# Block-local attention: the order in which SyncE moves keys, row maxima and queries of a group

## What is computed

```python
# B=8 batches, T=1024 tokens, C=128, H=16 heads of D=8, blocks of W=64 tokens, nb=16
q, k, v = (x @ Wq.T), (x @ Wk.T), (x @ Wv.T)       # split in 16 heads, 16 blocks of 64
k2 = concatenate([previous block of k, kb], axis=3) # 128 keys for 64 queries
v2 = concatenate([previous block of v, vb], axis=3)
base = (j > i) & (j <= i + W)                       # a sliding window of 64
scores = einsum('bhnqd,bhnkd->bhnqk', qb, k2) * D ** -0.5
p = softmax(where(mask, scores, -1e30), axis=-1)
out = einsum('bhnqk,bhnkd->bhnqd', p, v2)
x = x + out @ Wo.T
```

## Time and profile before

| | |
|---|---|
| median of 3 runs | 1809.45 us (1808.23 to 1809.67) |
| the profiled execution | 1814.3 us, of which the span is 1812.5 us |
| granted TensorE clock, mean of the span | 0.967 |
| PE busy | 1670.4 us, 92% of the span |
| DVE, ACT, POOL busy | 1393.8, 1137.5, 1177.3 us |
| the attention stage | from 73.6 us (first scores) to about 480 us |

### The profile page before, as it was taken

One profiled execution on the slowest core, in us unless ns is written; L12 is line 12 of the kernel. 1 busy time (PEld: TensorE's weight loads), 2 busy tenths in 40 slices (PEclk: granted clock), 3 DMA queues, 4 the chain that ended last, 5 costly groups with the idle time before them and its releaser, 6 DMA issues.

```text
span 1812.5 us, 39662 instructions
## 1 busy us (share of the span) xinstructions
PE 1670.4 (92%) x15057; PEld 1223.0 (67%) x15057; DVE 1393.8 (77%) x2976; ACT 1137.5 (63%) x2222; POOL 1177.3 (65%) x909
## 2 busy tenths in 40 slices
PE   4679999999877899999999999999999999999995
PEld 4557777777766567666766766766676677677674
DVE  5557777766597888878888888888887888888862
ACT  5447777777676466666666666666656666665662
POOL 4300111000066498898898988989889898898892
PEclk9889999999887899999999999999999999999997
DMA  4556666654000000000000000001001000100101
GB/s 123 136 140 156 162 156 159 164 136 116 29 1 1 1 10 8 10 8 10 7 13 16 10 8 19 11 7 22 7 10 19 8 10 7 22 7 10 19 10 30
DMA packets 198677, 81.47 MB, mean 45 GB/s; under 512 B 152553, under 2 KB 177493, under 8 KB 198357
## 3 DMA queue, kind: packets, MB, share of 16 engines
q1 hardware_dynamic: 198484, 78.93, 19.5%
HBM read 39.79 MB, written 29.88 MB: 38 GB/s over the span
## 4 chain that ended last, share of the span: by engine, by line
PE 54%; DVE 11%; POOL 2%; issue 1%; ACT 1%; DMA 0%; SPq 0%; POOLq 0%; ACTq 0%
PE pair L1825 12%; PE pair L1878 11%; PE pair L1882 11%; PE pair L1936 10%; DVE amax L1833 4%; PE pair L1929 4%; PE pair L1650 2%; DVE o_inv L1946 1%; PE pair L1641 1%; DVE stats L485 1%; POOL w_mix L1907 1%; PE pair L1664 1%; DVE q_low L1754 1%; DVE cq L1765 1%; DVE key_hl L1768 1%
## 5 line engine op out<-in xcount | busy, mean ns | idle before, releaser
L1893 ACT ACTIVATE prob<-pair 128x512 f32<-128x512 f32 x1024 | 604.4, 597 | 422.2 <-PE pair L1882 359.6
L1833 DVE TENSOR_REDUCE amax<-pair 128x1 f32<-128x512 f32 x1024 | 670.3, 682 | 133.9 <-PE pair L1825 131.8
L1825 PE MATMUL pair<-key_hl,q_hi 128*128 128x512 f32 x1024 | 437.8, 430 | 11.2 <-DVE amax L1833 7.1
L1878 PE MATMUL pair<-q_hi,key_hl 128*128 128x512 f32 x1024 | 405.2, 396 | 2.6 <-ACT prob L1893 2.6
L1882 PE MATMUL pair<-q_low,key_h 65*128 65x512 f32 x1024 | 406.0, 396 | 0.0
L1907 POOL TENSOR_TENSOR w_mix<-w_mix,prob 128x1024 f32<-128x1024 f32 x160 | 382.3, 2389 | 25.2 <-ACT prob L1893 8.5
L1907 POOL TENSOR_TENSOR Wm<-Wm,prob 128x1024 f32<-128x1024 f32 x155 | 369.6, 2384 | 20.8 <-ACT prob L1893 4.1
L520 POOL TENSOR_SCALAR veps<-mv 128x8 f32<-128x8 f32 x47 | 11.4, 243 | 452.6 <-DVE mv L493 451.2
L1825 PEld LDWEIGHTS pair<-key_hl,q_hi 128*128 128x128 f32 x1024 | 196.1, 192 | 115.9 <-issue 51.0
L1936 PE MATMUL pair<-prob,values 128*32 128x256 f32 x4096 | 247.2, 382 | 0.0
L1186 DVE TENSOR_REDUCE mx_neg<-pair 128x4 f32<-128x512 f32 x256 | 164.9, 687 | 94.8 <-PE pair L1090 94.1
(11 more groups left out here) (209 smaller groups left out, 2232.8 us busy)
## 6 DMA issues: line engine op xcount, KB each, us to landing
rows_mem<-once SPq DMA_DIRECT2D x128, 128.0 KB, 2.0
queries<-rows_mem SPq DMA_DIRECT2D x64, 256.0 KB, 4.5
keys<-rows_mem SPq DMA_DIRECT2D x16, 1024.0 KB, 7.1
rows_mem<-once SPq DMA_DIRECT2D x128, 64.0 KB, 1.9
q_low<-shift_cols SPq DMA_DIRECT2D x512, 0.5 KB, 2.0
yT<-o_norm SPq DMA_DIRECT2D x256, 32.0 KB, 1.9
x<-x_dram SPq DMA_DIRECT2D x8, 512.0 KB, 7.3
out_dram<-x SPq DMA_DIRECT2D x7, 512.0 KB, 3.4
```

The source lines that it names most:

```text
L1825: e.matmul(row_bank(("row", r, i)), q_hi[:, k, t * P:(t + 1) * P], key_hl[:, b % 2, i * HALF:(i + 1) * HALF], start=True, stop=True, skip_ ...
L1833: e.tensor_reduce(amax1[:, u % 2, t, i:i + 1], row_bank(("row", r, i)), AX_X, ALU.max).then_inc(*row_maxed.up((r, i)))
L1878: e.matmul(bank(j), key_hl[:, b % 2, ks], q_hi[:, k, sl], start=True, stop=False, skip_group_check=True)
L1893: e.activation(prob1[:, g % P_BUFS, half * HALF:(half + 1) * HALF], bank(K_BANKS[(2 * g + half) % 3]), ACT.Exp, scale=SCALE1).then_inc(*ke ...
```

## The change

Four edits.

- `window_plan`: of the two `once` parts of a group the keys' (i = 1) comes first, and the queries' (i = 0) second. The places in the plan stay.
- `sync`: for each hb now the spread and the gather of keys, then the maxima of group hb-2, then the spread and the gather of queries. For hb = 2 the maxima of group 0 come ahead of the keys. The loop runs one turn longer, so that the last maxima are moved.
- `sync_gather`: for keys of batch 2 and above, the wait names the last key rows that read the half that is overwritten. For half 1 (odd hb) that is the last step of group hb-4, as before; for half 0 (even hb) it is the first step of group hb-3, where it was that group's last.
- `opening`: the same swap for group 0.

```diff
@@ window_plan
-        [("turn", 0, 0), ("turn", 0, 1), ("once", 0, 0), ("once", 0, 1), ("v", 0, 0)])]
+        [("turn", 0, 0), ("turn", 0, 1), ("once", 0, 1), ("once", 0, 0), ("v", 0, 0)])]
...
-            first += [("once", after, i) for i in range(2)]
+            first += [("once", after, i) for i in (1, 0)]
@@ sync_gather
             elif b >= 2:
-                e.wait_ge(*key_rows.at(2 * HB * (2 * (b - 2) + 2) - 1))
+                e.wait_ge(*key_rows.at(2 * (HB * (hb - 4) + (HB if half == 0 else HB - 1)) + 1))
@@ sync
-            for hb in range(2 * B + 1):
+            for hb in range(2 * B + 2):
+                if hb == 2:
+                    sync_move_maxima(e, 0)
                 if hb < 2 * B:
-                    for i in range(2):
-                        sync_spread(e, hb, i)
-                    for i in range(2):
-                        sync_gather(e, hb, i)
-                if hb:
-                    sync_move_maxima(e, hb - 1)
+                    sync_spread(e, hb, 1)
+                    sync_gather(e, hb, 1)
+                if hb > 2:
+                    sync_move_maxima(e, hb - 2)
+                if hb < 2 * B:
+                    sync_spread(e, hb, 0)
+                    sync_gather(e, hb, 0)
```

## The result

The changed kernel takes 1924.48 us, the median of 4 runs (1912.33 to 1930.86), against 1808.84 us (1808.01 to 1809.67) for the kernel before: 1.0621 times as long, 95% interval 1.0587 to 1.0655. That is 115.6 us more, where 93 were forecast. The time lies inside the range of 1868 to 1935.

The account below looks back on a forecast made before the run. TensorE was taken to bound the kernel, busy 1670.4 of 1812.5 us. 12 x (6.2 + 2.9) = 109.2, less 4.0, 10.6 and 2.9, plus 1.4, gave +93 us: 1903 us, range 1868 to 1935.

Parts of the forecast that it names:

- The mechanism: On SyncE's queue maxima come behind keys' spread, landing and gather; TensorE waits in third steps, clock falls; +93 us, chance 0.80.
- The rival that the new order costs by itself: Not in the prediction; follow-up theory that early keys and swapped products slow the attention stage: above 1850 us; no chance given.
- The side of the gain: Rival: keys land before each group's start, so their waits and clock losses go; about 1787 or 1796 us; chance 0.05.
- the waits: TensorE's third step, groups 4 to 15: 12 waits for maxima of 6.2 us each, bounds 5.3 and 8.0.
- the clock: Behind each wait for maxima TensorE runs at the low level, costing 2.9 us; bounds 0 and 3.3.
- groups 1 and 2: At these groups' starts each spread has its own landing wait: 1.4 us lost together, bounds 0 and 3.
- the short waits: VectorE gets ahead during long waits, which takes perhaps 4 of the 5.8 us of TensorE's short waits away.
- waits for keys gone: TensorE's waits for keys of groups 4 to 15 disappear: 10.6 us won.
- the fifth step of the example: At group 5, four maxima moves follow the keys' gather and land at 208.6 to 209.2; 208.9 us taken.
- The other steps: SyncE at group 5: wait for `once`, eight spreads (4.06 us), landing 2.0 us from issue, keys' gather issue 1.26 us.
- My argument that both waits above 2.7 us were followed by it: Against the rival without clock loss (chance 0.08, about 1867 us): waits of 4.18 and 2.73 us preceded the low level.
- the rival: Worse than the high end: queries also land after the next group's start, using 7 us slack; above 1935 us; chance 0.04.

Follow-up runs that it names:

- both_spreads: Changed kernel with SyncE's order per group made maxima first, then the keys' and queries' spreads, then both gathers; 1811.39 us, 1.0013 of the kernel before.
- pool_moves: Changed kernel's order of keys and queries on SyncE, but GpSimd issues the four moves of each group's maxima; 1820.38 us, 1.0067 of the kernel before.
- pool_before: Kernel before with one change: GpSimd, not SyncE, moves the maxima; queries first, both spreads ahead of both gathers; 1806.48 us, ratio 0.9966.
- maxima_first: Changed kernel with the maxima of group hb-2 ahead of the keys of group hb for every hb, queries last; 1844.93 us, 1.0193 of the kernel before.
- maxima_landed: Changed kernel with the maxima moved after the landing of the keys' spread and ahead of the keys' gather; 1884.19 us, 1.0403 of the kernel before.
- pool_best: Changed kernel with GpSimd moving the maxima, and both spreads ahead of both gathers for groups 0 to 2; 1813.19 us, 1.003 of the kernel before.
- act_moves: Changed kernel's order of keys and queries on SyncE, but ScalarE issues the maxima's moves after copying them; 1832.82 us, 1.0118 of the kernel before.

## Why the prediction was right, and which terms were off

The mechanism was right: twelve waits, in each group's third step, for maxima that stand behind the keys' spread, landing and gather, and the low clock behind each. The rival that the new order costs by itself has only a small part: keys first costs nothing (both_spreads, 1.0013), and the change's whole order of spreads and gathers, with the maxima taken out of the queue, costs 11 of the 116 us (pool_moves, 1.0067). The side of the gain needed the keys' part to be through before the maxima were due; it began only 0.7 us after they were ready. The sum, 93, was a fifth below the 115.6 us measured: its three terms of cost (the waits, the clock, groups 1 and 2) were all too small, and only the short waits, where the gain was too small, went the other way. The mean wait lay inside its bounds; the clock and groups 1 and 2 did not. The sizes, term by term, against the 115.0 us between the two spans:

| term | forecast | measured | |
|---|---|---|---|
| 12 waits for the maxima | 74.4 | 88.9 | 7.4 us each, not 6.2 |
| clock, less group 12's old loss | 31.9 | 39.4 | more busy time of the same matmuls |
| waits for keys gone | -10.6 | -11.0 | 9.4, 0.4 for maxima and 1.2 at group 15 |
| short waits gone | -4.0 | -7.6 | 5.0 and 3.7 before, 1.1 after |
| groups 1 and 2 | 1.4 | 5.1 | group 3's start |
| sum | 93.1 | 114.8 | |

- **The wait: the fifth step of the example was too short.** I had the maxima land 5.3 us after the issue of the keys' gather, with the keys there after 5.2 us by the lone load. They came 6.2 to 7.0 us after it (304.07 to 310.28, and 233.65 to 240.64 at group 5's place), 6.5 in the mean of the twelve. That is the whole difference of 1.2 us. The keys themselves landed after 5.3 to 6.0 us, mean 5.6, which is near the load; the last of the four moves could be used 0.9 us behind them in the mean, while I let the two end together. The other steps were good to some tenths: spread 298.47 to 302.56, landing wait 1.5 us.
- **Short waits**: those on VectorE fell by 4.1 us, as forecast. The 3.5 us on ScalarE's `yT` that went with them are the part that I had not counted.
- **The clock** cost (39.4 + 2.9) / 12 = 3.5 us a wait, group 12's old loss counted in, where I took 2.9 and 3.3 as the upper end. Its price varies. Read in stretches of 1 us, the low level went on for 12.9 to 13.2 us behind five of the twelve waits (groups 3, 4, 5, 6 and 9), and for 3.2 to 5.6 us behind the other seven, 7.9 us in the mean, where I had said about 6. These are the stretches after group 4's wait and after group 7's:

```profile
202.98:209.00 6.02, 6.02 (x64) 4.85 (x65) 1.29 (x2) 3.52 (x8) 0.00 (x0) 0.50 0.56 135
209.00:216.00 7.00, 7.00 (x68) 5.30 (x66) 3.20 (x10) 3.70 (x10) 0.00 (x0) 0.50 0.45 91
...
310.28:316.00 5.72, 5.72 (x66) 4.51 (x66) 1.21 (x2) 2.09 (x4) 0.00 (x0) 0.59 0.61 146
316.00:322.00 6.00, 6.00 (x92) 5.24 (x91) 5.14 (x15) 4.37 (x11) 0.00 (x0) 1.00 0.51 105
```

  The changed kernel's four runs differ by 18.5 us. The four of the kernel before beside them differ by 1.7, but the 19 runs of it in the comparison with pool_before differ by 14.4, so that this says little. The mean granted clock goes with the time (0.932 in the run of 1931 us, 0.931 in that of 1929, 0.938 in that of 1920 and 0.939 in that of 1912), but which waits made the difference stays open, since only one of the runs has a profile with these rows. Nor does the length of a wait alone decide: 2.73 us at group 12 of the kernel before was followed by the low level, 3.25 us at group 8 of maxima_first by 1.00 from 284.2 to 290.0 us. My argument that both waits above 2.7 us were followed by it rested on two rows.
- **Groups 1 and 2**: I counted a separate landing wait of 2 us for the queries' spread. It was longer, since that spread stands behind the keys' gather. In the changed kernel, at group 1 (SyncE's timeline):

```profile
81.56 0.56 SPq L949 DMA_DIRECT2D keys<-rows_mem  x1
...
86.58 0.44 SPq L933 DMA_DIRECT2D rows_mem<-once  x1
90.23 1.96 SPq L953 DMA_DIRECT2D queries<-rows_mem  x3
```

  The queries' gather began at 90.23 and not at 88.9, and TensorE began the group at 97.34, not 96.4. Group 2 loses 2.8 us more, so that the two together are well beyond the upper bound of 3 that I gave. From group 4 on this delay was hidden behind the longer stage, as forecast: no wait for queries is left there. (The slack that I gave them there is 5.4 us by my own numbers, 221.6 to 227, and not the 7 that the rival names.)

The errors of the wait and of groups 1 and 2 share one thing, which I weighed for the maxima and did not follow up: the maxima and the queries' spread, both issued behind the gather of the keys, landed after its megabyte in the places shown.

## What to carry to other kernels

In a hand-ordered DMA queue, place each transfer by its deadline, and not by when its data are ready: four moves of 8 KB with 5 us to spare were put behind nine DMAs with a landing in between, and that was most of the 6%. A transfer that goes through memory and back pays its landing wait in the queue, so put another transfer's issues into that gap, and keep small or latency-bound transfers ahead of large ones. Where a queue is short of room, look for an idle engine that can issue the urgent ones; here GpSimd could, with both spreads ahead of both gathers, at a gain of 0.3%; with ScalarE, which TensorE waits for, the time rose by 1.2%.

## What the runs showed of the hardware

- Small DMAs issued behind a large one on the same queue came late: from the first of four 8 KB moves' issue to use it took 5.87 instead of 3.74 us in the mean of twelve places, behind 1 MB (the changed kernel and maxima_landed); and a spread of eight DMAs behind 1 MB had landed 4.5 us after its last issue (pool_best), instead of 2.0.
- Issuing four 8 KB DMAs took SyncE 2.4 to 3.3 us in the changed kernel, 2.53 at most places, ScalarE 3.1 us (act_moves, 204.56), and GpSimd 2.1 us. Its timeline in pool_best has:

```profile
197.55 2.08 POOL L973 DMA_DIRECT2D queries<-mx_rows  x4 [4.39 <-ACT mx_rows L1106]
```

- After each of the twelve waits of 6.5 to 9.1 us TensorE's granted clock was at its lower level, 0.50, for 3.2 to 5.6 us of full work at seven places and 12.9 to 13.2 us at five, in one and the same execution.
